# A tile's three weighted one-hots made by three VectorE operations, none by ScalarE

## The reference, cut to what matters

```python
norm = edge_weight * rsqrt(deg_out[src] * deg_in[dst] + EPS)
msg = (h @ W)[src] * norm[:, None]
agg = segment_sum(msg, dst, num_segments=n_nodes)   # dst is sorted
```

## Time and profile before

| what | value |
|---|---|
| median of 3 runs | 3784.66 us (3770.18 to 3797.39) |
| the profiled execution's own time | 3778.15 us |
| its span, first to last instruction | 3776.3 us |
| TensorE busy, share of the span | 2967.6 us, 79% |
| VectorE busy | 1996.9 us, 53% |
| ScalarE busy | 1383.0 us, 37% |
| GpSimd busy | 1990.4 us, 53% |
| mean granted TensorE clock | 0.897 |

### The profile page before, as it was taken

How to read it: one execution, slowest core, us unless ns; L and a number is a source line. 1 busy time by engine, 2 the same in 40 slices (tenths; PEclk the granted TensorE clock), 3 DMA queues, 4 the chain that set the end, 5 groups by cost and what they waited for, 6 DMA issues and landing times.

```text
span 3776.3 us, 58472 instructions
## 1 busy us (share of the span) xinstructions
PE 2967.6 (79%) x17257; PEld 2010.6 (53%) x17257; DVE 1996.9 (53%) x7494; ACT 1383.0 (37%) x3657; POOL 1990.4 (53%) x2006
## 2 busy tenths in 40 slices
PE   4577289999999999996768988888888654588885
PEld 3456145555555555564445655555555422477775
DVE  7999877777767767761202333333334353433332
ACT  5577355555555555542300111111111110255443
POOL 0000177555655555564467777777777773133332
PEclk9979699999999999998889998899999855799998
DMA  3001355555455555447546666666666643233334
GB/s 102 0 18 36 91 169 158 161 160 158 133 160 159 162 162 163 157 140 235 152 138 192 213 217 207 206 203 200 194 202 202 219 129 83 53 60 58 58 58 107
DMA packets 208605, 535.62 MB, mean 142 GB/s; under 512 B 42924, under 2 KB 138436, under 8 KB 202052
## 3 DMA queue, kind: packets, MB, share of 16 engines
q0 software_dynamic: 105936, 263.26, 28.4%
q1 hardware_dynamic: 100084, 260.60, 19.5%
q10 hardware_dynamic: 2304, 8.39, 0.6%
HBM read 380.42 MB, written 158.05 MB: 143 GB/s over the span
## 4 chain that ended last, share of the span: by engine, by line
PE 27%; POOL 23%; issue 15%; DMA 13%; DVE 13%; ACT 5%; DVEq 2%; SPq 1%; POOLq 0%; ACTq 0%
POOL arena L797 21%; PE bank L1706 9%; DMA acc<-arena 7%; PE bank L1698 7%; DMA sorted_x<-arena 4%; DVE arena L934 3%; ACT arena L1444 3%; PE bank L1720 2%; PE bank L1847 2%; DVE arena L1104 2%; PE bank L1730 2%; PE bank L1732 2%; PE bank L1857 1%; POOL sorted_x L805 1%; ACT arena L1452 1%
## 5 line engine op out<-in xcount | busy, mean ns | idle before, releaser
L797 POOL DMA_INDIRECT arena<-table,src_i x1792 | 1720.9, 960 | 862.0 <-issue 514.5
L1706 PE MATMUL bank<-arena 128*128 128x257 f32 x4704 | 1209.4, 392 | 6.2 <-ACT zcd L1461 6.2
L1706 PEld LDWEIGHTS bank<-arena 128*128 128x128 f32 x4704 | 870.9, 195 | 234.8 <-issue 114.1
L1452 ACT ACTIVATE arena<-arena 128x128 bf16<-128x128 bf16 x1440 | 487.2, 393 | 325.1 <-DVE arena L1086 318.6
L1698 PE MATMUL bank<-arena 128*128 128x343 bf16 x2160 | 459.3, 325 | 174.4 <-ACT arena L1452 90.9
L1104 DVE TENSOR_TENSOR arena<-arena,bank 128x343 f32 x720 | 366.2, 509 | 362.5 <-PE bank L1698 273.0
L1720 PE MATMUL bank<-arena,s_all 128*32 128x257 f32 x3584 | 285.1, 443 | 183.3 <-DMA arena<-table,src_i 168.6
L1698 PEld LDWEIGHTS bank<-arena 128*128 128x128 bf16 x2160 | 188.2, 99 | 416.3 <-DVE arena L1104 172.3
L844 POOL DMA_INDIRECT acc<-arena x105 | 168.3, 1603 | 343.4 <-ACT arena L1560 250.3
L1435 ACT COPY zs<-bank 128x257 f32<-128x257 f32 x224 | 83.2, 371 | 607.8 <-PE bank L1720 594.1
L1670 PE MATMUL bank<-arena 128*128 128x150 bf16 x1616 | 184.6, 273 | 112.0 <-DVE arena L934 107.3
(11 more groups left out here) (216 smaller groups left out, 3401.9 us busy)
## 6 DMA issues: line engine op xcount, KB each, us to landing
chunks<-arena SPq DMA_DIRECT2D x24, 3307.5 KB
arena<-chunks SPq DMA_DIRECT2D x24, 3307.5 KB, 13.4
arena<-table,src_i POOLq DMA_INDIRECT x1792
zsum<-zc SPq DMA_DIRECT2D x224, 64.2 KB
arena<-sorted_x SPq DMA_DIRECT2D x105, 132.5 KB, 2.1
zrow<-zsum SPq DMA_DIRECT2D x50, 257.0 KB, 4.5
arena<-in_W ACTq DMA_DIRECT2D x16, 512.0 KB, 15.2
arena<-in_x SPq DMA_DIRECT2D x5, 1280.0 KB, 12.7
```

The source lines that it names most:

```text
L797: pool.indirect_dma_start(gat[:, r, j, :], None, table[L], bass.IndirectOffsetOnAxis(ap=src_i[:, col:col + 1], axis=0)).then_inc(gathered[ ...
L1452: last = act.activation(parts[:, r, i], ohl[:, r], ACT.Copy, scale=w3f[:, i, t:t + 1])
L1706: last = pe.matmul(ps_ap, adj[:, c % 2, h, 0:P], xp[:, h], start=(h == 0), stop=(h == XB_ALL - 1))
```

## The change

`tile_one_hots` no longer makes `ohl`. It makes all three parts itself, each by one `tensor_scalar` with two per-partition operands (compare with the low bits, multiply by the part of the weight), in the form that `parts[0]` had. `tile_parts` is gone from ScalarE, and with it the semaphore `parts_made` and TensorE's wait for it. The buffer of `ohl` leaves the arena, so what lies behind it moves by its size.

```diff
--- before.py
+++ after.py
@@ -185,18 +185,16 @@
         OHK_W = OH_RING * (KEYS + 1) // 2
         PART_W = OH_RING * 3 * P // 2
         CM_W = 2 * (2 * GROWS)
-        OHL_W = OH_RING * P // 2
         OHG_W = TG * WIN // 2
         XP_W = XB_ALL * ROW
         A_W = 2 * XB_ALL * AWID
         DTX = DT
         SC_W = 5 * DTX
-        arena = sb("arena", [P, GAT_W + OHK_W + PART_W + CM_W + OHL_W + OHG_W + XP_W + A_W + SC_W])
+        arena = sb("arena", [P, GAT_W + OHK_W + PART_W + CM_W + OHG_W + XP_W + A_W + SC_W])
         o_ohk = GAT_W
         o_part = o_ohk + OHK_W
         o_cm = o_part + PART_W
-        o_ohl = o_cm + CM_W
-        o_ohg = o_ohl + OHL_W
+        o_ohg = o_cm + CM_W
         o_xp = o_ohg + OHG_W
         o_a = o_xp + XP_W
         o_sc = o_a + A_W
@@ -211,7 +209,6 @@
 
         ohk = area(o_ohk, OHK_W).bitcast(BF16).rearrange("p (r n) -> p r n", r=OH_RING)[:, :, 0:KEYS]
         parts = area(o_part, PART_W).bitcast(BF16).rearrange("p (r i n) -> p r i n", r=OH_RING, i=3)
-        ohl = area(o_ohl, OHL_W).bitcast(BF16).rearrange("p (r n) -> p r n", r=OH_RING)
         xp = area(o_xp, XP_W).rearrange("p (h n) -> p h n", h=XB_ALL)
         adj = area(o_a, A_W).rearrange("p (a h w) -> p a h w", a=2, h=XB_ALL)
         key = area(o_sc, DTX)
@@ -378,7 +375,7 @@
         f_norm, f_T, f_xT, f_mm, f_feat = (sem(n) for n in ("f_norm", "f_T", "f_xT", "f_mm", "f_feat"))
         table_in = sems("table_in", 2)
 
-        onehot_made, parts_made, built, added = (sem(n) for n in ("onehot_made", "parts_made", "built", "added"))
+        onehot_made, built, added = (sem(n) for n in ("onehot_made", "built", "added"))
         zeroed, chunk_stored = sem("zeroed"), sem("chunk_stored")
         applied, zcd_ready, zd_stored, zk_in = (
             sems(n, 2) for n in ("applied", "zcd_ready", "zd_stored", "zk_in"))
@@ -1082,9 +1079,10 @@
             def tile_one_hots(t):
                 r = t % OH_RING
                 dve.tensor_scalar(ohk[:, r], iota_key[:, 0:KEYS], key[:, t:t + 1], None, ALU.is_equal)
-                dve.tensor_scalar(ohl[:, r], iota_b[:, :], lo_f[:, t:t + 1], None, ALU.is_equal)
-                dve.tensor_scalar(parts[:, r, 0], iota_b[:, :], lo_f[:, t:t + 1], w3f[:, 0, t:t + 1], ALU.is_equal,
-                                  ALU.mult).then_inc(onehot_made, 1)
+                for i in range(3):
+                    last = dve.tensor_scalar(parts[:, r, i], iota_b[:, :], lo_f[:, t:t + 1], w3f[:, i, t:t + 1],
+                                             ALU.is_equal, ALU.mult)
+                last.then_inc(onehot_made, 1)
 
             def tile_offsets(t):
 
@@ -1444,14 +1442,6 @@
                 act.copy(adj[:, c % 2, first:last], zero[:, :].unsqueeze(2).broadcast_to([P, last - first, AWID])
                          ).then_inc(zeroed, 1)
 
-            def tile_parts(t):
-
-                r = t % OH_RING
-                act.wait_ge(onehot_made, t + 1)
-                for i in (1, 2):
-                    last = act.activation(parts[:, r, i], ohl[:, r], ACT.Copy, scale=w3f[:, i, t:t + 1])
-                last.then_inc(parts_made, 1)
-
             def copy_chunk(L, c):
                 act.wait_ge(applied[L], 2 * c + 2)
                 if c > 1:
@@ -1598,13 +1588,9 @@
                 for c in range(2):
                     zero_chunk(c, 0, HALF_HI)
                     zero_chunk(c, HALF_HI, XB_ALL)
-                for t in range(OH_RING):
-                    tile_parts(t)
                 for it in range(LOOP_GROUPS // GPI):
                     for u in range(2 * CT):
                         c, step = chunk_slot(it, u)
-                        if it * 2 * CT + u + OH_RING < DT:
-                            tile_parts(it * 2 * CT + u + OH_RING)
                         if u - 1 in GROUP_AT:
                             copy_sums(0, it * GPI + GROUP_AT.index(u - 1))
                         if u - COMBINE_AFTER in GROUP_AT:
@@ -1693,7 +1679,6 @@
             def build_tile(t):
 
                 pe.wait_ge(onehot_made, t + 1)
-                pe.wait_ge(parts_made, t + 1)
                 for i in range(3):
                     last = pe.matmul(ps_b[t % 2], parts[:, t % OH_RING, i], ohk[:, t % OH_RING], start=(i == 0),
                                      stop=(i == 2))
```

## The result

The changed kernel takes 3787.1 us (median of 12 runs, 3781.5 to 3793.4), the kernel before, run beside it, 3782.7: a ratio of 1.0025, 95% interval 1.0013 to 1.0037, so 9.5 us slower, between 5 and 14. The medians as they stand differ by 4.4 us; the ratio compares fast executions alone, and one of the kernel before, at 3930.9 us, was in a slower state. The forecast was +6.

The account below looks back on a forecast made before the run. TensorE was taken as the bound at nine tenths, waiting mainly for VectorE. VectorE's lateness +18, ScalarE's wait -9, zeroing -5 and start +2 gave +6 on 3784.66: 3791 us, own range 3765 to 3822, 8 in 10 within 3762 to 3843.

Parts of the forecast that it names:

- Item 1: VectorE's queue per tile: two more operations 0.22 us apart replace ohl, so 1.315 us a tile in place of 1.03.
- Item 2: VectorE's operations stretched by neighbours: about 13 ns each, 0.05 us a tile for four.
- Item 3: VectorE late around two register loads per pair of chunks, by 0.5 and 1.2 us: +18 us, from below 0 to +57.
- The count of 50.7 of 51.6 us a chunk: VectorE's operations, groups, loads and stretches after the change: 50.7 us per 51.6 us chunk, fitting with nothing over.
- Item 4: TensorE's 17.3 us of waits for ScalarE's parts in the loop go; half taken, -9 us, ends 0 and -17.
- Item 5: ScalarE's zeroing at 22 chunk boundaries comes up to about 0.4 us earlier: -9 us at most, -5 taken.
- Item 6: Loop's start: first add up to 7.3 us earlier, but VectorE slower in the first chunks: +2 us, ends -7 and +9.
- The clock: TensorE's granted clock in the loop, 0.95 of full: longer pauses at boundaries might lower it, costed at nothing.
- Slower by the clock: Longer TensorE pauses at boundaries or long loads keep its clock low twice as long: +57, 3848 us; chance 0.10.
- Slower by the queue: VectorE's operations cost their whole duration, or lateness isn't absorbed between loads: about +52, 3837 us; chance 0.14.
- Faster: Two PSUM banks absorb VectorE's lateness and ScalarE's hold-ups are won in full: -33, 3752 us, or 3733; chance 0.11.
- Lock-out by GpSimd: Each added VectorE operation that meets a GpSimd gather waits for its rest: +190 us, 3975; chance 0.01.

Follow-up runs that it names:

- D: Kernel before, VectorE's queue filled as in the changed one (ohl in two-operand form, one more such operation), ScalarE still making its parts: 3816.9 us, ratio 1.0108.
- C: Kernel before without ScalarE's two parts per tile (left zero) and TensorE's wait for them, VectorE's queue untouched: 3753.9 us, ratio 0.9947.
- E: Changed kernel with registers loaded five at a time in place of ten: 3763.1 us, ratio to the kernel before 0.9963.
- G: Kernel before with registers loaded five at a time in place of ten: 3768.1 us, ratio 0.9977.
- the split: Kernel before with parts[0] and parts[1] made by VectorE, only parts[2] by ScalarE, on a slower chip: ratios 1.0081 and 1.0092, with loads of five 1.0079.

## Why the prediction was right, point by point

The forecast was +6 us and 3791; measured were +9.5 by the ratio and 3787.1. The signs stood: VectorE pays, ScalarE's share is won back, and the net is small. The sizes and the place did not, and it is in part luck that the total came out near. Both sides were too small and their errors cancelled; TensorE's busy time fell by 9.6 us, for which the sum had nothing; and 4.9 us of the difference of the two profiles lie behind the loop, where nothing changed. In the part that the sum was about, up to the last add, the profiles say +4.3 where it says +6.

- **What bounds the kernel.** "VectorE is what it waits for, and ScalarE is nearly no part of it" read the row of 75.7 us wrongly: 64.5 of them are the wait at a chunk's boundary, where VectorE itself waits for ScalarE's zeroing. Only 11.2 us had VectorE's own work behind them; ScalarE's zeroing and its parts stood behind the other 82 of TensorE's 93.
- **Item 1, 1.315 us a tile.** Right: 1.31 from add to add, and the distance of 0.22 holds for three like operations in a row.
- **Item 2.** The stretch is there, and small: a mean of 332 ns over the 2160 operations, against a median of 308. That is 24 ns where 13 were taken.
- **Item 3, VectorE's lateness, +18.** The mean load stretches of the changed kernel grew by 0.15 and 0.34 us a pair, 5 us in all; I had said 0.5 and 1.2. But with ScalarE's wait left in (D) they grew by 0.9 a pair, 10 us, and the whole of VectorE's side from tile 60 on was 25 (D against before) or 22 (changed against C). The step that failed is the one that cost the other stretches at nothing: in D 12 us are at the boundaries, and of the 22 of the changed kernel against C 15 are there (16.43 us in place of 15.74) and only 7 at the two loads. I had called their cover the zeroing and TensorE's low clock. It doesn't reach the four tiles behind a chunk's first add: there VectorE is the bound, as the prediction's paragraph on the clock says itself, and they take 1.02 us more a chunk.
- **The count of 50.7 of 51.6 us a chunk** said that VectorE's queue is nearly full. E fits it: with the standstill of the loads shorter by 42 us the loop is 22 us shorter, and 20 of them lie in the two load stretches.
- **Item 4, ScalarE's wait, -9 of 17.** C shows that the whole of it is won: the idle time of 17.3 us vanished, and the wait for the add stayed at 76.7. I had halved it for want of a reason that a row shows.
- **Item 5, the zeroing, -5.** The start at the boundary shown is 0.45 us earlier, about as predicted; in the mean of all it is 0.31, which is 7 us in place of the 5 taken. The waits fell by 7.0 us in C, and by 16.2 in the changed kernel, where part is VectorE's later arrival and so no gain.
- **Item 6, the start, +2.** The first add came 6.9 us earlier, as counted, and the first 60 tiles took 103.8 us in place of 93.6: +3.2 together.
- **The clock, at nothing.** It moved the other way than the rival feared: TensorE was busy 9 us less for the same instructions. The time at 1.2 GHz is 10 us shorter, which in TensorE's work is worth about 5 of them (an estimate: half); the rest isn't explained. E, the changed kernel with other loads, has the same low busy time, 1030.2 us, while C and D have 1038.9 and 1042.2, so it goes with the change; why isn't shown.
- **The rivals.** Slower by the clock: out. Slower by the queue: its first half (the lateness isn't absorbed) is what D shows with +41, but ScalarE's side pays it back. Faster: its ScalarE side, -33 with nothing on VectorE's, was -20 measured in C. Lock-out by GpSimd: out, the longest of the changed operations lasts 580 ns.

Open: the 4.9 us behind the loop. Behind its last add the profiled executions of before, changed, C, D, E and G took 2080.3, 2085.2, 2078.6, 2087.8, 2084.7 and 2089.1 us, all with the same code there. Before and G, which share even the arena, lie 8.8 us apart, so 4.9 is within what such executions differ by; that it is scatter and nothing else isn't shown. The other layout of the arena wasn't tested by itself: C and D keep the old one.

## What to carry to other kernels

An engine with 70% of busy time can have a full queue: count it from start to start, with register loads and waits in it, before giving it work. Sort the waits by where in the loop they lie and follow each one engine further: a row "TensorE waits for VectorE" was here mostly ScalarE's zeroing. A mean over a chunk hides the tiles in which the neighbour has nothing else to do, and these pay first. When work moves from one engine of a chain to another, measure each side by itself, one with the work left out and one with the work doubled; here a change of +9 us hid -20 and +41. Where the queue is full, making its stops shorter (five registers a load in place of ten) was worth more on the first chip than where the work lies: E is 0.37% faster than before, and the fastest kernel here that computes the whole result.

## What the runs showed of the hardware

- A register load of ten values takes 1.06 us at least and 2.30 in the median, one of five 0.585 and 1.184, one of two 0.52 and 0.53. The longest of the kernel before, 3.93 us, ran from 1560.38 to 1564.30 while VectorE worked off until 1561.69 what had been issued before; the next add started at 1564.53.
- A `tensor_scalar` on 128 columns of bf16 with two per-partition operands lasts 308 ns and the next starts 0.22 us behind it; with one such operand `ohl` in the earlier trace rows leaves the queue after 0.16.
- The same program took 3778 us on one chip and 4318 to 4420 on another. The variants traced there have the same median durations of their instructions. Of the 245 us by which the split's loop is longer than that of the kernel before on the first chip, 45 are TensorE's busy time, at a granted clock of 0.93 in place of 0.95, and 200 are time in which it stood still.
